# A causal mask moved: from a TensorE matmul into the score bank to a predicated copy on VectorE behind the exp

## The chip, the cores and the metric

The kernel runs on one NeuronCore of a Trainium2 chip. The metric is the time of one execution on the device in microseconds (us). The kernel before took 2042.52 us as the median of 3 runs (2041.71 to 2043.63).

## What is computed

One transformer block on a sequence of 2048 tokens of width 512, in float32: LayerNorm, attention with 32 query heads in 8 groups (4 query heads share one key and one value head, head size 64), residuals, LayerNorm, and a feed-forward part with ternary weights. The part that the change touches is this:

```python
q = _rope(q)
k = _rope(k)
qk = jnp.einsum('bghsd,bgxpd->bghsp', q, k) * DQK ** (-0.5)
causal = jnp.tril(jnp.ones((s, s), dtype=bool))
qk = jnp.where(causal, qk, -jnp.inf)
attn = jax.nn.softmax(qk, axis=-1)
o = jnp.einsum('bghsp,bgxpd->bghsd', attn, v)
```

## The kernel before, in words

There are four stages: `normalise` (to about 76 us), `attention` (about 76 to 1510 us), `output_projection` and `feed_forward`. The change lies in `attention` alone. Float32 values are split into a high and a low 16-bit half, and each product is made from several 16-bit matmuls.

**Tiling.** `attention` runs over 8 groups of heads. A group has 16 units: 4 chunks c of 512 queries, times 4 heads h. A unit has one step for each tile of 128 keys that its queries may see, so 4(c+1) steps; a group has 160 steps. In the last four steps of a unit (j = 4c to 4c+3) the key tile meets the queries on the diagonal: step 4c+r has only the query tiles r to 3, so 512, 384, 256 or 128 columns, and its first 128 columns need the causal mask. That makes 64 diagonal steps in a group: steps 0 to 15 (all of chunk 0), 20 to 23, 28 to 31, 36 to 39, 44 to 47 (chunk 1), 56 to 59, 68 to 71, 80 to 83, 92 to 95 (chunk 2), 108 to 111, 124 to 127, 140 to 143 and 156 to 159 (chunk 3). Over 8 groups there are 1280 steps, 512 of them diagonal.

**One step i.** TensorE makes the transposed scores (keys on partitions, queries on columns) in one of 2 score banks with two matmuls (L569, L570). In a diagonal step a third matmul (L573) adds, over 128 columns, `big` (30000 times the identity) times `mask_kq` (-30000 where key > query). ScalarE waits for that and writes the exp as float32 to `p32`, a ring of 10 (`exps`, L637). The upper 16 bits of each float32 are read in place as bfloat16 (`p_high`). GpSimd subtracts them and writes the float16 rest to `pl` (`low_part`, L789). TensorE multiplies both with the values (`values`, L586, L588, L590: three matmuls of 65, 64 and 65 columns for each query tile).

**Side work.** A softmax needs the row's maximum before its exp. TensorE makes the scores a second time, with queries on partitions, one piece of up to 512 columns a step (`max_piece`, L554), into 4 side banks in turn; VectorE reduces each piece (`reduce_piece`: L704 for whole pieces, L708 with the causal mask for those on the diagonal). Projections of later tokens (`project`, L541, 12 matmuls of 384 columns) share the 4 side banks; VectorE takes them out (`out_of_bank`, L727 to L733), GpSimd finishes rope and the low half (L795, L804). TensorE may write a side bank only when VectorE has read the item that was there four items before (`take_bank`).

**Order.** Every engine runs its own instructions in order. The order is written out by hand as slots, one for each step: in slot n TensorE does `scores(n)`, the slot's first piece, `values(n-5)`, and a projection if the slot has one (`JOB_STEPS`: among others slots 4, 8, 12 and 16). One slot later in the program order VectorE does its part: `unit_low`, `reduce_piece` of the slot, `unit_out`, `out_of_bank`. GpSimd does `low_part(n)`, then the rest of the projection's work. The first three steps of the next group (HEAD = 3) are scored at the end of a group, between the last three `values`, and their exp and `low_part` stand at the end of the slots; VectorE has `unit_out(15)` there. So in slot 3 of a group steps 0 to 2 are already done.

Of the kernel before, what the change touches and what calls it, by code (L numbers as in the profile page):

```python
# [226 lines left out]
    return max(0, j - TPC * c)  # L227


def score_bank(i):  # L230

    return i % SBANKS
# [110 lines left out]
def attention(nc, w_in_t, w_out_t, attn_dram, yh, yl, consts, cos, sin, wraw, wh, wl, wscale, raw, z_out):  # L343
# [6 lines left out]
    with ExitStack() as ctx:  # L350
        sb = lambda name, shape, dt: ctx.enter_context(nc.sbuf_tensor(name, shape, dt))
        sem = lambda name: ctx.enter_context(nc.semaphore(name))
        ident16, big, mask_kq, mask_qk = (consts[:, i, :] for i in range(4))
        rope_a = sb("rope_a", [P, TILES_KEPT, HG + 1, DH], F32)
        rope_b = sb("rope_b", [P, TILES_KEPT, HG + 1, DH], F32)
        qk_hi = sb("qk_hi", [P, 2, HG + 1, TPC, 2, DH], F16)
# [10 lines left out]
        o_hl = sb("o_hl", [P, 2, 2, TPC, HG, DH], F16)  # L367
        o_turn = sb("o_turn", [P, 2, 2, TPC, 2 * P], F16)
        credit = sb("credit", [P, 16], F32)
        causal = sb("causal", [P, CHUNK], BF16)  # L370
        masked = sb("masked", [P, 2, CHUNK], BF16)
        ps = ctx.enter_context(nc.psum_tensor("a_ps", [P, 8, 512], F32))
# [25 lines left out]
        maxs_used = sem("maxs_used")  # L398
        m_ready = sem("m_ready")
        exp_done = sem("exp_done")  # L400
        low_ready = sem("low_ready")
        pv_done = sem("pv_done")
        o_scaled = sem("o_scaled")
# [110 lines left out]
        def _(pe):  # L514
            pe.wait_ge(ones_set, 2)
            def group(g, par, part):
# [41 lines left out]
                def scores(i, ahead=0):  # L558
                    gg, side = g + ahead, par ^ ahead
                    u, j = step_of(i)  # L560
                    c, h = divmod(u, HG)
                    if j == 0:
                        pe.wait_ge(lm_in[c % 2][h], 16 * (2 * gg + c // 2 + 1))
                    pe.wait_ge(exp_done, gg * STEPS + bank_before(i) + 1 + EXP_AHEAD)
                    r = first_query_tile(c, j)
                    diag = j >= TPC * c
                    keys = slice(j * P, (j + 1) * P)
                    out = sbank(i)[:, r * P:CHUNK]
                    nc.tensor.matmul(out, k_hl[:, side, keys], q_hh[:, c % 2, h, r * P:CHUNK], start=True, stop=False)  # L569
                    last = nc.tensor.matmul(out, k_h1[:, side, keys], q_lm[:, c % 2, h, r * P:CHUNK],  # L570
                                            start=False, stop=not diag)
                    if diag:
                        last = nc.tensor.matmul(sbank(i)[:, r * P:(r + 1) * P], big, mask_kq, start=False, stop=True)  # L573
                    last.then_inc(scores_ready, 1)

                def values(i):
                    u, j = step_of(i)
# [103 lines left out]
        def _(dve):  # L681

            nc.vector.memset(v[:, :, :, DH:DH + 1], 1.0).then_inc(ones_set, 1)
            nc.vector.memset(causal[:, 0:CHUNK - P], 0.0)
            nc.vector.tensor_scalar(causal[:, CHUNK - P:CHUNK], mask_qk, LEAST / 3e4, None, ALU.mult).then_inc(causal_set, 1)
            dve.wait_ge(causal_set, 1)
# [4 lines left out]
            def group(g, par, part):  # L691
# [5 lines left out]
                def reduce_piece(ahead, u, i):  # L697
                    gg, (c, h), n = g + ahead, divmod(u, HG), FIRST_STEP[u] + i
                    t, kk = divmod(i, c + 1)
                    width = CHUNK if kk < c else (t + 1) * P  # L700
                    dve.wait_ge(maxs_ready, gg * PIECES + n + 1)
                    bank = side_bank(part, ("piece", ahead, u, i))[:, 0:width]
                    if kk < c:
                        nc.vector.reduce_max(mpart[:, u % 2, t, kk:kk + 1], bank, AX.X).then_inc(maxs_used, 1)  # L704
                    else:
                        if ahead or n >= 2:
                            dve.wait_ge(maxs_used, gg * PIECES + n - 1)
                        nc.vector.tensor_tensor_reduce(masked[:, n % 2, 0:width], bank, causal[:, CHUNK - width:CHUNK], 1.0, -LEAST,  # L708
                                                       ALU.add, ALU.max, mpart[:, u % 2, t, kk:kk + 1]).then_inc(maxs_used, 1)
                    if i < KEY_TILES[u] - 1:  # L710
                        return

                    dve.wait_ge(maxs_used, gg * PIECES + n + 1)
                    if ahead or c >= 2:
                        dve.wait_ge(lm_in[c % 2][h], 16 * (2 * gg + c // 2))
                    nc.vector.reduce_max(qk_lo[:, c % 2, h, :, 1, 0:1].rearrange("p t a -> p (t a)"),
                                         mpart[:, u % 2, :, 0:c + 1], AX.X).then_inc(m_ready, 1)

                def out_of_bank(ahead, t):
                    gg, side, b = g + ahead, par ^ ahead, t % TILES_KEPT  # L720
# [31 lines left out]
                for n in range(len(part) + 1):  # L752
                    step, _, pieces = slot(part, n - 1)
                    if step is not None and step - LOW_OUT_LAG in FIRST_STEP:
                        unit_low(FIRST_STEP.index(step - LOW_OUT_LAG) - 1)
                    for piece in pieces[:1]:
                        reduce_piece(*piece)
                    if step is not None and step - PV_LAG in FIRST_STEP[1:]:
                        unit_out(FIRST_STEP.index(step - PV_LAG) - 1)
                    for piece in pieces[1:]:  # L760
                        reduce_piece(*piece)
                    if step is not None:
                        if step in W_SPLIT and part is SLOTS:
                            weights_low(1, W_SPLIT[step])
                    if job := slot(part, n - OUT_OF_BANK_LAG)[1]:
                        out_of_bank(*job[1:])
                if part in (SLOTS, FINAL):
                    unit_out(UNITS - 1)
                if part is LAST:
# [6 lines left out]
        @block.gpsimd  # L776
        def _(pool):

            nc.gpsimd.memset(qk_lo[:, :, 0:HG, :, 1, :], 0.0).then_inc(rows_set, 1)
            nc.gpsimd.memset(qk_hi[:, :, HG, :, 1, 1:DH], 0.0).then_inc(rows_set, 1)  # L780
            nc.gpsimd.memset(qk_hi[:, :, HG, :, 1, 0:1], -1.0).then_inc(rows_set, 1)
            pool.wait_ge(ones_set, 2)
            def group(g, par, part):
                def low_part(i, ahead=0):
                    u, j = step_of(i)
                    r = first_query_tile(u // HG, j)
                    cols = slice(r * P, CHUNK)
                    pool.wait_ge(exp_done, (g + ahead) * STEPS + i + 1 + EXP_AHEAD)
                    nc.gpsimd.tensor_tensor(pl[:, i % RING, cols], p32[:, i % RING, cols], p_high[:, i % RING, cols],  # L789
                                            ALU.subtract).then_inc(low_ready, 1)  # L790

                def rope_sum(ahead, t):
                    b = t % TILES_KEPT
                    pool.wait_ge(rope_parts, (g + ahead) * TT + t + 1)
                    nc.gpsimd.tensor_tensor(rope_a[:, b], rope_a[:, b], rope_b[:, b], ALU.add).then_inc(roped_ready, 1)  # L795

                def qk_low_part(ahead, t):
                    (c, tt), gg = divmod(t, TPC), g + ahead
                    pool.wait_ge(qk_high, gg * TT + t + 1)
                    if tt == 0 and (ahead or c >= 2):  # L800
                        for h in range(HG):
                            pool.wait_ge(lm_in[c % 2][h], 16 * (2 * gg + c // 2))
                        pool.wait_ge(k_in[(c - 2) % NCH], 32 * (gg + (c >= 2)))
                    nc.gpsimd.tensor_tensor(qk_lo[:, c % 2, :, tt, 0, :], rope_a[:, t % TILES_KEPT], qk_hi[:, c % 2, :, tt, 0, :],  # L804
                                            ALU.subtract).then_inc(qk_low, 1)

                for n in range(len(part) + 2):
                    step = slot(part, n - 1)[0]
                    if step is not None:
                        if step >= HEAD:  # L810
                            low_part(step)
                    if job := slot(part, n - QK_LOW_LAG)[1]:
                        qk_low_part(*job[1:])
                    if job := slot(part, n - SUM_LAG)[1]:
                        rope_sum(*job[1:])
                for i in range(HEAD if part in (OPENING, SLOTS) else 0):
                    low_part(i, ahead=int(part is SLOTS))

            group(0, 0, OPENING)
            every_group(group)  # L820
# [400 lines left out]
def build(nc, x, w_in_t, w_out_t, rms_w, ffn_t, cos_dram, sin_dram, ident_dram, half_consts, out):  # L1221
    resid = nc.dram_tensor("resid_scratch", (S, D), F32, kind="Internal").ap()
    attn = nc.dram_tensor("attn_scratch", (2, TT, P, CT, P), F16, kind="Internal").ap()
    with nc.sbuf_tensor("raw", [P, NW], F32) as raw, nc.sbuf_tensor("ident_sb", [P, P], F32) as ident:
        with ExitStack() as ctx:
# [1 line left out]
            z_out = ctx.enter_context(nc.semaphore("z_out"))  # L1227
            yh = sb("yh", [P, KT, S], F16)
            yl = sb("yl", [P, KT, S], F16)
            consts = sb("consts", [P, 4, P], F16)  # L1230
            cos = sb("cos_sb", [P, TT, DH], F32)
            sin = sb("sin_sb", [P, TT, DH], F32)
            wraw = sb("wraw", [P, KT, GC], F32)
# [23 lines left out]
def shape_constants():  # L1257
# [4 lines left out]
    cos, sin = np.cos(ang).astype(np.float32), np.sin(ang).astype(np.float32)  # L1262
    big = np.float16(30000.0)
    key, query = np.arange(P)[:, None], np.arange(P)[None, :]
    half = np.stack([np.eye(P), np.eye(P) * big, np.where(key > query, -big, 0), np.where(query > key, -big, 0)], axis=1)
    unit = np.float32(QK_SCALE / W_SCALE)
    return (np.concatenate([cos, cos], 1) * unit, np.concatenate([-sin, sin], 1) * unit, np.eye(P, dtype=np.float32),
            half.astype(np.float16))
# [24 lines left out]
```

## Time and profile before

| | before |
|---|---|
| median of 3 runs | 2042.52 us |
| the profiled execution itself | 2040.19 us |
| its span, first to last instruction | 2038.3 us |
| TensorE busy | 1935.4 us (95%) |
| GpSimd busy | 1421.2 us (70%) |
| VectorE busy | 1234.5 us (61%) |
| ScalarE busy | 932.2 us (46%) |
| mean granted TensorE clock | 0.983 of full speed |

Busy times are unions of the durations of an engine's instructions. A matmul's duration includes the way through the array, so consecutive matmuls overlap in the record; what a matmul costs in a dense stream is the distance from its start to the next one's. The same holds, to a smaller degree, for VectorE, whose next instruction starts a little before the last one ends. The profile's stretches of time below are of group 4, which runs from 801.90 us (its first `scores`, in the tail of group 3) to 978.55 us.

### The profile page before, as it was taken

The numbers are of one execution on the slowest core, as the hardware profiler recorded it, in microseconds if no ns is written. First come the engines' busy times: TensorE is split into PE (matmuls) and PEld (weight loads), VectorE is DVE, ScalarE is ACT, GpSimd is POOL, SyncE is SP. The second block draws the span as 40 slices with busy tenths as digits, with TensorE's granted clock in tenths as the row PEclk, the third lists the DMA queues.
The fourth block names the chain that finished last, engine by engine and source line by source line (L and its number), as shares of the span: only waits on it lengthen the run. The fifth ranks groups of instructions, "written<-read, shape, count | busy, mean of one in ns | idle before, by whom it ended". The sixth has DMA issues, their size and how long they took to land. (4 is left out here: it accounts for less than half of the span.)

```text
span 2038.3 us, 55132 instructions
## 1 busy us (share of the span) xinstructions
PE 1935.4 (95%) x21382; PEld 1184.9 (58%) x21382; DVE 1234.5 (61%) x3284; ACT 932.2 (46%) x1969; POOL 1421.2 (70%) x1627
## 2 busy tenths in 40 slices
PE   4799989999999999999999999999969998999998
PEld 3466656666666666666666666666634443444443
DVE  6587558757866875886687588668625552121221
ACT  4355645555655555565555556555632211121110
POOL 1599979989999998999899899999930001131221
PEclk8799999999999999999999999999989999999999
DMA  6233263223224322322522332242246620000000
GB/s 205 58 66 46 46 158 65 46 50 76 44 53 87 61 46 55 71 46 51 98 51 46 59 66 46 51 81 52 38 155 227 217 83 1 16 5 21 5 16 21
DMA packets 301572, 136.79 MB, mean 67 GB/s; under 512 B 248336, under 2 KB 285456, under 8 KB 299792
## 3 DMA queue, kind: packets, MB, share of 16 engines
q1 hardware_dynamic: 301328, 133.43, 28.5%
q8 instruction: 166, 2.72, 0.6%
q14 instruction: 78, 0.64, 0.1%
HBM read 49.48 MB, written 25.17 MB: 37 GB/s over the span
## 5 line engine op out<-in xcount | busy, mean ns | idle before, releaser
L789 POOL TENSOR_TENSOR pl<-p 128x512 f16<-128x512 f32 (+3 forms) x1280 | 1136.3, 919 | 108.2 <-ACT p L637 107.0
L637 ACT ACTIVATE p<-a_ps 128x512 f32<-128x512 f32 (+3 forms) x1280 | 674.3, 532 | 606.1 <-PE a_ps L570 384.4
L704 DVE TENSOR_REDUCE mpart<-a_ps 128x1 f32<-128x512 f32 x768 | 514.2, 685 | 117.6 <-PE a_ps L554 114.7
L586 PE MATMUL a_ps<-v,p 128*128 128x65 f16 x4352 | 527.7, 193 | 14.9 <-POOL pl L789 11.3
L588 PE MATMUL a_ps<-v,p 128*128 128x64 f16 x4352 | 530.1, 194 | 0.0
L590 PE MATMUL a_ps<-v,pl 128*128 128x65 f16 x4352 | 526.9, 192 | 0.0
L586 PEld LDWEIGHTS a_ps<-v,p 128*128 128x128 bf16 x4352 | 412.1, 97 | 121.6 <-issue 16.8
L588 PEld LDWEIGHTS a_ps<-v,p 128*128 128x128 bf16 x4352 | 405.8, 97 | 103.2 <-issue 0.2
L554 PE MATMUL a_ps<-k_hl,q_hh 128*128 128x512 f16 (+3 forms) x1280 | 441.3, 350 | 24.6 <-issue 12.4
L569 PE MATMUL a_ps<-q_hh,k_hl 128*128 128x512 f16 (+3 forms) x1280 | 444.4, 347 | 2.5
L570 PE MATMUL a_ps<-q_lm,k_h 128*128 128x512 f16 (+3 forms) x1280 | 444.8, 347 | 0.0
L590 PEld LDWEIGHTS a_ps<-v,pl 128*128 128x128 f16 x4352 | 407.1, 99 | 0.0
L708 DVE CUSTOM_DVE_ANT_0 masked<-a_ps,causal 128x128 bf16<-128x128 f32 (+3 forms) x512 | 247.1, 484 | 81.5 <-PE a_ps L554 73.8
L1218 POOL TENSOR_TENSOR f_hl<-f_hid,f_hh 128x512 f16<-128x512 f32 x64 | 74.1, 1160 | 240.1 <-DVE f_hh L1188 240.1
L554 PEld LDWEIGHTS a_ps<-k_hl,q_hh 128*128 128x128 f16 x1280 | 124.0, 98 | 144.2 <-issue 16.9
L1133 PE MATMUL f_ps<-xh,tern 128*128 (+1 forms) x512 | 195.1, 381 | 1.8 <-DVE f_credit L1175 1.8
L1133 PE MATMUL f_ps<-xl,tern 128*128 (+1 forms) x512 | 195.0, 381 | 0.0
L541 PE MATMUL a_ps<-wh,yh 128*128 128x384 f16 x512 | 168.7, 329 | 8.6 <-DVE credit L690 8.6
L944 PE MATMUL p_ps<-p_wh,p_att 128*128 128x512 f16 x512 | 156.1, 381 | 14.9 <-DMA p_att<-attn_scratch 14.9
L541 PE MATMUL a_ps<-wl,yh 128*128 128x384 f16 x512 | 168.6, 329 | 0.0
L541 PE MATMUL a_ps<-wh,yl 128*128 128x384 f16 x512 | 168.4, 329 | 0.0
L1169 ACT ACTIVATE f_silu<-f_ps,tern_scale 128x512 f32<-128x512 f32 x64 | 44.0, 687 | 256.8 <-PE f_ps L1133 256.8
(96 smaller groups left out, 2268.2 us busy)
## 6 DMA issues: line engine op xcount, KB each, us to landing
attn_scratch<-o_turn SPq DMA_DIRECT2D x64, 256.0 KB, 2.8
p_att<-attn_scratch SPq DMA_DIRECT2D x32, 512.0 KB, 4.3
raw<-ffn_t SPq DMA_DIRECT2D x12, 1024.0 KB, 5.0
wraw<-w_in_t SPq DMA_DIRECT2D x8, 768.0 KB, 5.0
resid_scratch<-raw SPq DMA_DIRECT2D x4, 1024.0 KB, 4.3
raw<-w_out_t SPq DMA_DIRECT2D x1, 4096.0 KB, 16.8
x<-resid_scratch SPq DMA_DIRECT2D x4, 1024.0 KB, 7.5
out<-x SPq DMA_DIRECT2D x16, 256.0 KB, 2.1
```

Source lines behind the costliest of these rows:

```text
L541: last = nc.tensor.matmul(bank[:, 0:GC], a[:, kt, tok], b[:, kt, :], start=(kt == 0 and n == 0), stop=(kt == KT - 1 and n == 2))
L554: nc.tensor.matmul(bank[:, 0:width], q_hh[:, c % 2, h, t * P:(t + 1) * P], k_hl[:, par ^ ahead, kk * CHUNK:kk * CHUNK + width], start=True ...
L569: nc.tensor.matmul(out, k_hl[:, side, keys], q_hh[:, c % 2, h, r * P:CHUNK], start=True, stop=False)
L570: last = nc.tensor.matmul(out, k_h1[:, side, keys], q_lm[:, c % 2, h, r * P:CHUNK], start=False, stop=not diag)
L586: nc.tensor.matmul(o, weights, v[:, par, j, 0:VU], start=(j == 0 and t == 0), stop=False, skip_group_check=True)
L588: nc.tensor.matmul(o[:, 0:DH], weights, v[:, par, j, VL:VW], start=False, stop=False, skip_group_check=True)
L590: last = nc.tensor.matmul(o, pl[:, i % RING, t * P:(t + 1) * P], v[:, par, j, 0:VU], start=False, stop=(j == TPC * c + t), skip_group_chec ...
L637: nc.scalar.activation(p32[:, i % RING, r * P:CHUNK], sbank(i)[:, r * P:CHUNK], ACT.Exp, scale=SCALE).then_inc(exp_done, 1)
L704: nc.vector.reduce_max(mpart[:, u % 2, t, kk:kk + 1], bank, AX.X).then_inc(maxs_used, 1)
L708: nc.vector.tensor_tensor_reduce(masked[:, n % 2, 0:width], bank, causal[:, CHUNK - width:CHUNK], 1.0, -LEAST, ALU.add, ALU.max, mpart[:, ...
L789: nc.gpsimd.tensor_tensor(pl[:, i % RING, cols], p32[:, i % RING, cols], p_high[:, i % RING, cols], ALU.subtract).then_inc(low_ready, 1)
L1133: last = nc.tensor.matmul(bank, w[:, k, e * P:(e + 1) * P], x[:, k, bass.ds(c * CHUNK, CHUNK)], start=(k == 0 and x is xh), stop=(k == KT ...
```

## The change

The identity and `big` leave the constants, and so does the mask matmul of the diagonal steps. VectorE gets a tile of zeros, and for each diagonal step a predicated copy, `causal_cut`, which waits for the exp of the step and writes zeros to the 128 columns of `p32` where key > query (the predicate is the bit pattern of `mask_kq`, read as uint16). It stands in VectorE's order after `unit_low` and ahead of the slot's first `reduce_piece`; those of steps 0 to 2 stand after the slots, ahead of `unit_out(15)`. GpSimd's `low_part` of a diagonal step waits for the copy as well as for the exp. TensorE's `values` has no new wait: it waits for `low_part` already.

```diff
+def on_diagonal(i):
+    u, j = step_of(i)
+    return j >= TPC * (u // HG)
+
+def cuts_to(i):
+    return sum(on_diagonal(n) for n in range(i + 1))
+
+DIAGONALS = cuts_to(STEPS - 1)
...
-        ident16, big, mask_kq, mask_qk = (consts[:, i, :] for i in range(4))
+        mask_kq, mask_qk = (consts[:, i, :] for i in range(2))
...
+        zeros = sb("zeros", [P, P], F32)
+        future = mask_kq.bitcast(mybir.dt.uint16)
...
-                    diag = j >= TPC * c
...
-                    last = nc.tensor.matmul(out, k_h1[:, side, keys], q_lm[:, c % 2, h, r * P:CHUNK],
-                                            start=False, stop=not diag)
-                    if diag:
-                        last = nc.tensor.matmul(sbank(i)[:, r * P:(r + 1) * P], big, mask_kq, start=False, stop=True)
-                    last.then_inc(scores_ready, 1)
+                    nc.tensor.matmul(out, k_h1[:, side, keys], q_lm[:, c % 2, h, r * P:CHUNK],
+                                     start=False, stop=True).then_inc(scores_ready, 1)
...
+                def causal_cut(i, ahead=0):
+                    r = first_query_tile(step_of(i)[0] // HG, step_of(i)[1])
+                    dve.wait_ge(exp_done, (g + ahead) * STEPS + i + 1 + EXP_AHEAD)
+                    nc.vector.copy_predicated(p32[:, i % RING, r * P:(r + 1) * P], future, zeros[:, :]).then_inc(cut, 1)
...
                     if step is not None and step - LOW_OUT_LAG in FIRST_STEP:
                         unit_low(FIRST_STEP.index(step - LOW_OUT_LAG) - 1)
+                    if step is not None and step >= HEAD and on_diagonal(step):
+                        causal_cut(step)
                     for piece in pieces[:1]:
                         reduce_piece(*piece)
...
+                for i in range(HEAD if part in (OPENING, SLOTS) else 0):
+                    if on_diagonal(i):
+                        causal_cut(i, ahead=int(part is SLOTS))
                 if part in (SLOTS, FINAL):
                     unit_out(UNITS - 1)
...
                     pool.wait_ge(exp_done, (g + ahead) * STEPS + i + 1 + EXP_AHEAD)
+                    if on_diagonal(i):
+                        pool.wait_ge(cut, (g + ahead) * DIAGONALS + cuts_to(i))
                     nc.gpsimd.tensor_tensor(pl[:, i % RING, cols], p32[:, i % RING, cols], p_high[:, i % RING, cols],
                                             ALU.subtract).then_inc(low_ready, 1)
```

## Rows read from the trace of the kernel before

**Rows 1.** The page, busy time of engines, share of the span, instructions.
```profile
PE 1935.4 (95%) x21382; PEld 1184.9 (58%) x21382; DVE 1234.5 (61%) x3284; ACT 932.2 (46%) x1969; POOL 1421.2 (70%) x1627
```

**Rows 2.** Busy time by stretch: window, us, then busy us (instructions) of each engine.
```profile
804.00:820.00 16.00, 15.92 (x183) 10.65 (x181) 13.17 (x43) 8.43 (x24) 12.71 (x19) 1.00 0.32 61
820.00:835.00 15.00, 14.92 (x214) 10.28 (x213) 12.81 (x41) 10.46 (x25) 14.24 (x18) 1.00 0.40 89
835.00:880.00 45.00, 45.00 (x603) 30.00 (x601) 37.27 (x99) 26.64 (x61) 43.15 (x50) 1.00 0.42 78
880.00:963.70 83.70, 83.70 (x1138) 55.63 (x1137) 58.88 (x155) 46.47 (x98) 79.37 (x90) 1.00 0.22 38
963.70:981.00 17.30, 15.24 (x247) 10.54 (x246) 5.73 (x24) 10.56 (x24) 17.14 (x20) 1.00 0.52 99
```

**Rows 3.** Groups of instructions by line: busy, mean ns, idle before, releasers.
```profile
L789 POOL TENSOR_TENSOR pl<-p 128x512 f16<-128x512 f32 (+3 forms) x1280 | 1136.3, 919 | 108.2 <-ACT p L637 107.0
L573 PE MATMUL a_ps<-consts 128*128 128x128 f16 x512 | 112.5, 220 | 0.0
```

**Rows 4.** Timeline, TensorE: start us, us, instruction, idle before it.
```profile
802.33 0.22 PE L573 MATMUL a_ps<-consts 128*128 128x128 f16 x1
802.39 0.19 PE L586 MATMUL a_ps<-v,p 128*128 128x65 f16 x1
...
805.11 0.10 PEld L554 LDWEIGHTS a_ps<-k_hl,q_hh 128*128 128x128 f16 x1 [0.41 <-DVE mpart L704]
```

**Rows 5.** Timeline, VectorE in the normalisation, then at the group's start.
```profile
37.43 2.20 DVE L152 SCALAR_TENSOR_TENSOR wl<-wraw,wscale,wh 128x384 f16<-128x384 f32 x4
...
803.82 0.18 DVE L739 RECIPROCAL rden<-a_ps 128x4 f32<-128x4 f32 x1 [4.32 <-PE a_ps L590]
804.03 0.43 DVE L741 TENSOR_TENSOR a_ps<-a_ps,rden 128x256 f32<-128x256 f32 x1
804.38 0.68 DVE L704 TENSOR_REDUCE mpart<-a_ps 128x1 f32<-128x512 f32 x1
804.97 0.28 DVE L708 CUSTOM_DVE_ANT_0 masked<-a_ps,causal 128x128 bf16<-128x128 f32 x1
805.18 0.08 DVE L708 DVE_READ_ACCUMULATOR2_ANT mpart<- 128x1 f32 x1
805.18 0.69 DVE L704 TENSOR_REDUCE mpart<-a_ps 128x1 f32<-128x512 f32 x1
805.78 0.41 DVE L708 CUSTOM_DVE_ANT_0 masked<-a_ps,causal 128x256 bf16<-128x256 f32 x1
806.12 0.08 DVE L708 DVE_READ_ACCUMULATOR2_ANT mpart<- 128x1 f32 x1
```

**Rows 6.** VectorE's groups from 804 to 820 us, one row.
```profile
L727 DVE TENSOR_SCALAR v<-a_ps 128x64 f16<-128x64 f32 x3 | 0.7, 224 | 2.7 <-PE a_ps L541 2.7
```

**Rows 7.** Lines L694 and L152, durations min/median/max ns; timeline; GpSimd at 876.3, 877.5.
```profile
L694 DVE SCALAR_TENSOR_TENSOR wl<-wraw,wscale,wh x28: 710/818/1308, 151.2 to 1236.0; 128x384 f16<-128x384 f32 x28
...
L152 DVE SCALAR_TENSOR_TENSOR wl<-wraw,wscale,wh x4: 609/613/614, 37.4 to 39.0; 128x384 f16<-128x384 f32 x4
...
876.23 1.30 DVE L694 SCALAR_TENSOR_TENSOR wl<-wraw,wscale,wh 128x384 f16<-128x384 f32 x1
...
L789 POOL TENSOR_TENSOR pl<-p 128x512 f16<-128x512 f32 x1 | 1.0, 1035 | 0.0
...
L789 POOL TENSOR_TENSOR pl<-p 128x512 f16<-128x512 f32 x1 | 1.4, 1351 | 0.0
```

**Rows 8.** Timeline, GpSimd and ScalarE around the group's start and end.
```profile
802.59 1.52 ACT L637 ACTIVATE p<-a_ps 128x512 f32<-128x512 f32 x3 [3.04 <-PE a_ps L573]
...
803.26 3.75 POOL L789 TENSOR_TENSOR pl<-p 128x512 f16<-128x512 f32 x5 [0.17 <-ACT p L637]
808.43 0.83 POOL L789 TENSOR_TENSOR pl<-p 128x384 f16<-128x384 f32 x1 [1.42 <-ACT p L637]
...
813.42 0.83 POOL L789 TENSOR_TENSOR pl<-p 128x384 f16<-128x384 f32 x1 [1.42 <-ACT p L637]
...
963.70 1.04 POOL L789 TENSOR_TENSOR pl<-p 128x512 f16<-128x512 f32 x1 [0.72 <-ACT p L637]
...
971.01 8.74 POOL L789 TENSOR_TENSOR pl<-p 128x512 f16<-128x512 f32 x10
```

More of the change, by code:

```diff
@@ L400, in attention @@
         exp_done = sem("exp_done")
+        cut = sem("cut")
         low_ready = sem("low_ready")
@@ L683, in _ @@
             nc.vector.memset(v[:, :, :, DH:DH + 1], 1.0).then_inc(ones_set, 1)
+            nc.vector.memset(zeros[:, :], 0.0)
             nc.vector.memset(causal[:, 0:CHUNK - P], 0.0)
@@ L1229, in build @@
             yl = sb("yl", [P, KT, S], F16)
-            consts = sb("consts", [P, 4, P], F16)
+            consts = sb("consts", [P, 2, P], F16)
             cos = sb("cos_sb", [P, TT, DH], F32)
@@ L1264, in shape_constants @@
     key, query = np.arange(P)[:, None], np.arange(P)[None, :]
-    half = np.stack([np.eye(P), np.eye(P) * big, np.where(key > query, -big, 0), np.where(query > key, -big, 0)], axis=1)
+    half = np.stack([np.where(key > query, -big, 0), np.where(query > key, -big, 0)], axis=1)
     unit = np.float32(QK_SCALE / W_SCALE)
```

## The prediction

> **What bounds the kernel now.** I read the page's busy shares first [rows 1]: TensorE 95%, GpSimd 70%, VectorE 61% over the whole span. These are averages over stages, so the second view is busy time by stretch for one group of the attention [rows 2]. There TensorE is busy nearly all the time from 804 to 963.7 us, GpSimd is close behind it (12.71 + 14.24 + 43.15 + 79.37 = 149.47 of 159.7 us), and VectorE, harmless on the page, is busy 13.17 of 16.0 us and 12.81 of 15.0 us in the first two stretches, 83% of 31 us. The third view is the waits. GpSimd idles only for the exp, 108.2 us in all [rows 3], and each exp it waits for had itself waited for TensorE; it idles 1.42 us at 808.43 and at 813.42, after a projection has kept TensorE from scores [rows 8]. From 963.70 to the group's end GpSimd has no gap, with ten `low_part` in a row from 971.01 [rows 8], and TensorE is busy only 15.24 of 17.3 us [rows 2]. So a group is bound by TensorE for some 160 us and by GpSimd for the last 17 us. VectorE already touches TensorE once: at 805.11 the piece of slot 4 waits 0.41 us for the reduce that began at 804.38 [rows 4, 5].
>
> **What is removed.** 512 mask matmuls [rows 3]. Their recorded 220 ns is mostly the way through the array; in the stream one costs 802.39 - 802.33 = 0.056 us (to the rounding of these rows) [rows 4]. That is 64 x 0.056 = 3.6 us a group and 29 us in all if TensorE were the bound everywhere. The masks of steps 156 to 159 and 0 to 2 lie where GpSimd is the bound, so at most 57 x 0.056 = 3.2 us a group, 25.5 us in all. The exp's operand and time stay.
>
> **What VectorE gets.** The trace has no predicated copy. The nearest operation has both inputs in SBUF like it (zeros and predicate) and float32 in it: L152, four in 2.20 us with the last 0.613 us long, so one per (2.20 - 0.61)/3 = 0.53 us at 384 columns [rows 5, 7]. By columns: L708 takes 0.21 us to the next start at 128 and 0.34 us at 256 [rows 5], so 0.13 us for 128 columns, and 0.53 - 0.26 = 0.27 us at 128. The lower bound is the 0.21 us of L708. I take 0.27 us.
>
> **What the copy waits for.** The same operation as L152 runs in the attention as L694, beside a working GpSimd, and takes 710 to 1308 ns, median 818, where L152 takes 609 to 614 [rows 7]. The slowest kind shows how: L694 starts at 876.23 while GpSimd is in a subtraction of 1035 ns, ends at 877.53, and the next GpSimd subtraction takes 1351 ns, against 1035 for its neighbour. VectorE stood still until GpSimd's instruction ended, then GpSimd stood still until VectorE's ended. The mean of L694 is about 0.3 us over L152. A copy of 128 columns is as likely to meet a running GpSimd instruction, so the added wait lies between 0 (GpSimd idle, or the copy's operands don't meet GpSimd's) and 1.04 us (a whole L789), and I take 0.3 us where GpSimd is saturated. Where VectorE is late, GpSimd itself is waiting for the copy and partly idle, and I take 0.2 us. GpSimd loses 1351 - 1035 = 0.316 us to 384 columns; less 0.26 for the smaller width that is 0.05 us for each copy.
> The Trainium skill (SBUF — State Buffer, section Who interferes with whom) says that a VectorE instruction with two SBUF inputs contends with a GpSimd instruction that reads SBUF, the loser blocking for the whole instruction. This trace agrees (1305 and 1351 ns above). The page doesn't list the predicated copy there; if the rule holds for it, the sum below stands, and if not, the first rival does.
>
> **The sum for one group, by stretch.** VectorE's demand is its busy time [rows 2] plus the copies.
> (a) 804 to 820 us, slots 3 to 16, 13 copies. VectorE has 2.83 us idle, 2.7 of it waiting for projections [rows 6]. 13 x (0.27 + 0.2) = 6.1 us don't fit. Two things happen. First, copies 0 to 2 stand ahead of `unit_out(15)` and of slot 0's reduce. The exps of steps 0 to 2 run from 802.59 to 804.11 [rows 8], and copy 1 or 2 also meets GpSimd's subtractions of 1.04 us; so the reduce that began at 804.38 begins at about 805.7. TensorE was waiting for just that one in slot 4 [rows 4], so it loses 1.3 us directly. Second, VectorE falls behind by 0.27 + 0.2 us a diagonal slot and recovers in the projections; the four side banks let it be about 2 us late without harm. 13.17 + 6.1 = 19.3 us in 16; of the 3.3 us too much about 1.7 are carried. I take +1.6 us.
> (b) 820 to 835 us, slots 17 to 31, 8 copies, GpSimd busy 14.24 of 15: 12.81 + 8 x 0.57 = 17.4 us, +2.4 us.
> (c) 835 to 880 us, 16 copies: 37.27 + 16 x 0.57 = 46.4 us of 45, +1.4 us, part of it the lag carried in.
> In (a) to (c) VectorE is the bound, and the masks' 0.056 us come back as longer waits of TensorE.
> (d) 880 to 963.7 us, 20 diagonal steps: 58.88 + 20 x 0.57 = 70.3 us of 83.7, it fits. GpSimd 79.37 + 20 x 0.05 = 80.4, it fits too. TensorE saves 20 x 0.056 = 1.1 us: -1.1 us.
> (e) 963.7 to 981 us, GpSimd's stretch, 7 copies: VectorE is idle two thirds of it and makes the copies in time (GpSimd lags the exp), but each costs GpSimd 0.05 us, and `low_part(0)`, which waited 0.17 us for the exp [rows 8], now waits for a copy behind it: +0.5 us.
> Together 1.6 + 2.4 + 1.4 - 1.1 + 0.5 = +4.8 us a group, times 8 = +38 us. The profiled execution took 2040.2 us (span 2038.3 and 1.9 around it), so 2078.6; the runs' median lies 2.3 us above it: 2081 us.
>
> **What costs nothing.** The smaller constants, the memset of the zeros before the first group, the removed weight loads (beside matmuls). ScalarE's exp starts 0.056 us sooner, which only lengthens GpSimd's backlog.
>
> **Rivals.**
> 1. The copy doesn't meet GpSimd's reads: no 0.2 to 0.3 us. Then (a) 13.17 + 3.5 = 16.7 us of 16 with a carry, so 0 to +0.7; (b) 12.81 + 2.2 = 15.0 of 15, 0; (c) 37.27 + 4.3 = 41.6 of 45, -0.9; (d) -1.1; (e) 0. That is -1.3 to -2.0 us a group, up to the -3.2 us of all masks: 2017 to 2032, about 2028 us. For it: VectorE has 39% idle on the page, and only L694, 28 instructions, speaks for the blocking. Against: L694 is never as fast as L152 in 28 cases. It decides from about 0.1 us of blocking for each copy: then (a) and (b) give 1.3 + 0.7 us back, as much as (c) and (d) save.
> 2. TensorE's saving and VectorE's lateness cancel, or GpSimd swallows both: GpSimd has only 159.7 - 149.5 = 10 us of gaps in the 160 us that TensorE bounds, and where it has none (820 to 835 us) a faster TensorE gains nothing. 2038 to 2047, about 2043 us.
> 3. The blocking is worse than L694's mean, since GpSimd's next instruction is always the one that has just been released: 0.6 us. Then (a) +4, (b) 12.81 + 7.0 = 19.8, +4.8, (c) 37.27 + 13.9 = 51.2, +6.2, (d) -1.1, (e) +1: +15 us a group, 2162 us at the extreme. Against: a VectorE that late leaves GpSimd idle, which ends the blocking. I take 2115 us and up as this case.
> That the mask isn't applied as said is no rival: the copy is issued once for each diagonal step.
>
> **Chances.** My case (VectorE becomes the bound in the first half of a group) 0.62, of itself 2050 to 2112; rival 1 0.22; rival 2 0.08; rival 3 0.08. Faster by over 0.2% (what can be told from no change here, 4 us): 0.22. Within: 0.08. Slower: 0.70. The range must reach into rival 1: 2030 to 2112 leaves out about half of it and rival 3.
>
> **What would show it.** Right: the predicated copy's row has a mean well over 0.28 us and a maximum near 1.3 us; TensorE's L554 has a wait for VectorE's L704 or L708 of some us a group, most in slots 4 to 31, where it is 0.41 us at one place now; VectorE's idle before L727 shrinks; GpSimd waits for the copy instead of the exp in the first 20 us of a group; the stretch from step 0 to step 72 grows by 5 us and that from 880 to 963.7 shrinks by 1. Wrong: copies of 0.2 to 0.3 us without spread (rival 1), or a slow group whose lost time lies in GpSimd's stretch at the end, which I price at 0.5 us, or a longer time with VectorE idle in slots 0 to 31: then the new wait for the exp in VectorE's queue, not its load, is the cause.

## The result, and the profile after

The kernel after takes 2091.82 us (median of 4 runs, 2089.49 to 2096.55); the kernel before took 2042.12 us beside it. The ratio is 1.0249, with a 95% interval of 1.0230 to 1.0268: 49.7 us slower. The prediction was 2081 us, in a range of 2030 to 2112, with a chance of 0.70 for slower. The profiled execution took 2089.49 us, its span 2087.7 us.

The page's first part and the two groups that answer to [rows 1] and [rows 3] (busy us, mean ns of one, idle before, releaser):

```profile
PE 1927.7 (92%) x20870; PEld 1155.9 (55%) x20870; DVE 1443.1 (69%) x3797; ACT 929.2 (45%) x1969; POOL 1442.5 (69%) x1627
...
L816 POOL TENSOR_TENSOR pl<-p 128x512 f16<-128x512 f32 (+3 forms) x1280 | 1150.3, 925 | 135.6 <-DVE p L737 69.4
...
L737 DVE COPY_PREDICATED p<-consts,zeros 128x128 f32<-128x128 uint16 x512 | 275.2, 539 | 83.7 <-ACT p L650 80.8
```

TensorE has 512 matmuls less and is busy 7.7 us less; the time is 50 us more, so it waits more. VectorE is busy 208.6 us more (0.41 us for each copy), and GpSimd idles 27 us more in front of its subtractions, now half of the time for the copy. A copy takes 539 ns on average, though 128 columns are short work. The durations of that line (min/median/max) show a wide spread:

```profile
L737 DVE COPY_PREDICATED p<-consts,zeros x512: 287/459/1192, 77.7 to 1540.1; 128x128 f32<-128x128 uint16 x171
```

Busy time by stretch in group 4, cut at the same steps as [rows 2] (window, length, then TensorE, its weight loads, VectorE, ScalarE, GpSimd, granted clock):

```profile
826.30:843.90 17.60, 16.20 (x177) 10.56 (x176) 17.34 (x57) 8.29 (x24) 13.20 (x18) 1.00 0.24 47
843.90:860.40 16.50, 14.74 (x199) 9.19 (x197) 15.71 (x46) 9.99 (x24) 16.50 (x21) 1.00 0.35 74
860.40:908.20 47.80, 44.68 (x584) 28.96 (x584) 45.07 (x116) 26.71 (x61) 42.10 (x49) 1.00 0.43 76
908.20:992.70 84.50, 83.07 (x1117) 54.69 (x1116) 67.69 (x180) 46.49 (x98) 80.65 (x90) 1.00 0.20 38
992.70:1011.60 18.90, 16.47 (x239) 10.93 (x238) 8.36 (x30) 10.60 (x24) 17.47 (x21) 0.91 0.45 92
```

Where TensorE was busy without a break it now is not, and VectorE is busy 17.34 of 17.60 us, 15.71 of 16.50 us and 45.07 of 47.80 us: up to about step 72 it has next to no room. In the second stretch GpSimd has none at all (16.50 of 16.50 us), so there busy time doesn't say which of the two is the bound. The longest waits of TensorE in the first and the third stretch of group 4 are one in slot 4, which the prediction named, and one in slot 32, which it did not (timeline, idle time before in brackets):

```profile
828.70 0.39 PE L571 MATMUL a_ps<-k_hl,q_hh 128*128 128x512 f16 x1 [1.40 <-DVE mpart L718]
...
861.83 0.38 PE L571 MATMUL a_ps<-k_hl,q_hh 128*128 128x512 f16 x1 [2.28 <-issue]
```

The first is the wait that was 0.41 us long in [rows 4] on the weight load, and was said to grow by 1.3 us. The second has no name in the view. The last key transpose before it was issued at 859.26 us and landed 2.5 us later, and the matmul starts 0.09 us after the landing:

```profile
k_hl<-qk_lo SPq DMA_TRANSPOSE x1, 2.5
```

In all eight groups this piece starts 0.09 us after that landing, after a wait of 2.28 to 3.51 us. In groups 1 to 6 it is 2.98 us on average; in the kernel before, it was 0.83 us on average, and nothing in group 4. VectorE ahead of the wait in slot 4, to be laid beside [rows 5]:

```profile
825.66 0.31 DVE L737 COPY_PREDICATED p<-consts,zeros 128x128 f32<-128x128 uint16 x1 [2.66 <-ACT p L650]
826.15 1.36 DVE L737 COPY_PREDICATED p<-consts,zeros 128x128 f32<-128x128 uint16 x2 [0.19 <-ACT p L650]
827.42 0.17 DVE L759 RECIPROCAL rden<-a_ps 128x4 f32<-128x4 f32 x1
827.62 0.43 DVE L761 TENSOR_TENSOR a_ps<-a_ps,rden 128x256 f32<-128x256 f32 x1
827.97 0.68 DVE L718 TENSOR_REDUCE mpart<-a_ps 128x1 f32<-128x512 f32 x1
```

The reciprocal stood at the head of VectorE's queue; now three copies do, which wait for the exps (2.66 and 0.19 us) and, the last two, for GpSimd (1.36 us for two).

A table of the whole, from the starts of the exps of the steps named, mean of groups 1 to 6, in us. The four later columns are the difference to before:

| steps | before | after | no_mask_matmul | aside_load_only | copies_late_only |
|---|---|---|---|---|---|
| 3 to 16 | 16.96 | +1.10 | -0.78 | +0.09 | -0.13 |
| 16 to 32 | 15.57 | +1.53 | 0.00 | -0.01 | +0.01 |
| 32 to 72 | 45.85 | +2.69 | -0.87 | +1.27 | +0.04 |
| 72 to 145 | 82.67 | +0.80 | -0.77 | +0.99 | -0.61 |
| 145 to 3 of the next | 18.11 | +0.28 | -0.18 | 0.00 | +0.01 |
| sum | 179.16 | +6.39 | -2.60 | +2.34 | -0.68 |

Within 72 to 145, the kernel after is +1.40 in steps 72 to 84 and -0.61 in 84 to 144. Not every row is the same in each group. In steps 3 to 16 the kernel after loses 1.54 us in four of the six groups, group 4 among them, and nothing in group 1. In steps 32 to 72 the losses of single groups of one kernel lie up to 3.7 us apart, so a mean there is worth less than one in another row. The +0.28 of the last row is 0.05 or less in five groups and 1.57 in group 4, where the granted clock fell (see the end).

### The profile page after: what moved, and what is told of

The parts are those of the page before. It is cut to its first block and busy times, and to the rows that moved or that the text cites. A ratio compares the mean times of both kernels' runs of the same rounds, so it can differ in the third digit from the quotient of the medians.

```text
span 2087.7 us, 55133 instructions
## 1 busy us (share of the span) xinstructions
PE 1927.7 (92%) x20870; PEld 1155.9 (55%) x20870; DVE 1443.1 (69%) x3797; ACT 929.2 (45%) x1969; POOL 1442.5 (69%) x1627
## 5 line engine op out<-in xcount | busy, mean ns | idle before, releaser
L816 POOL TENSOR_TENSOR pl<-p 128x512 f16<-128x512 f32 (+3 forms) x1280 | 1150.3, 925 | 135.6 <-DVE p L737 69.4
L718 DVE TENSOR_REDUCE mpart<-a_ps 128x1 f32<-128x512 f32 x768 | 506.9, 681 | 38.7 <-PE a_ps L571 37.3
L737 DVE COPY_PREDICATED p<-consts,zeros 128x128 f32<-128x128 uint16 x512 | 275.2, 539 | 83.7 <-ACT p L650 80.8
```

The costliest lines, as they stand in the source:

```text
L737: nc.vector.copy_predicated(p32[:, i % RING, r * P:(r + 1) * P], future, zeros[:, :]).then_inc(cut, 1)
```

## The experiments

The theory under test: a copy makes VectorE late, by its load and most of all by standing blocked behind GpSimd's running instruction; TensorE then waits for side banks. The rivals were that GpSimd's new wait for the copy costs the time, and that the wait for the exp at the head of VectorE's queue does. Each kernel was timed beside the kernel before (2041.49 us in the first four, 2041.56 in the next four, 2040.57 in the next three, 2039.74 in the last).

### One SBUF input instead of two

```diff
-nc.vector.copy_predicated(p32[:, i % RING, r * P:(r + 1) * P], future, zeros[:, :]).then_inc(cut, 1)
+nc.vector.reduce_max(aside[:, i % 16:i % 16 + 1], p32[:, i % RING, r * P:(r + 1) * P], AX.X).then_inc(cut, 1)
```

> The kernel after, with the predicated copy replaced by a max-reduce of the same 128x128 float32 tile of p32 into a spare column: same place in VectorE's order, same waits for the exp, GpSimd still waits for it, but one SBUF input instead of two and hardly a write. The mask is left out of the weights. Theory (the copy is blocked behind GpSimd's running instruction): each takes about 0.28 us without spread, GpSimd's 128x512 subtractions have none of 1.08 to 1.09 us beside it, and the time falls from 2092 to 2030-2050 us. Rival (the load of 512 more instructions and their wait for the exp at the head of VectorE's queue cost the time, whatever the operands): 2075-2095 us.

Measured: 2059.17 us, ratio 1.0080 (1.0063 to 1.0097). The operation in the copy's place:

```profile
L737 DVE TENSOR_REDUCE aside<-p x512: 266/278/288, 77.0 to 1512.6; 128x1 f32<-128x128 f32 x171
its engine sat idle before it (us, times) until:
  ACT p L650: 98.0, 110
```

No spread, as the theory said, and 32.7 us of the kernel's time are gone. But the time missed my 2030 to 2050: 17.7 us over before are left, and against the kernel without masks (2022.06) even 37.1. Load and waits cost more than I gave them. The reduce also writes only one column, so this run alone doesn't say whether the second input or the wide write made the copy wait. The kernel after has an operation that does: the first product of rope reads PSUM and one SBUF input, and writes 320 float32 columns to SBUF.

```profile
L749 DVE TENSOR_TENSOR rope_a<-a_ps,cos_sb x128: 473/481/483, 49.0 to 1443.0; 128x320 f32<-128x320 f32 x128
```

Of these 128, 103 started while a GpSimd instruction ran (95 of them a `low_part`), and none is longer than 483 ns. So a wide float32 write beside GpSimd costs nothing here, and what the blocked operations share (the copy, and the weight split of [rows 7]) is the second SBUF input.

### No mask at all

```diff
-                    if diag:
-                        last = nc.tensor.matmul(sbank(i)[:, r * P:(r + 1) * P], big, mask_kq, start=False, stop=True)
```

> The kernel before with the 512 mask matmuls left out and nothing in their place, so the scores of the weights have no causal mask. It prices what the change can save on TensorE. Theory: TensorE bounds about 57 of 64 diagonal steps of a group, but GpSimd has few gaps there, so 1.3 to 2.5 us a group of the possible 3.6: 2022-2032 us. Rival (GpSimd swallows it): 2038-2043 us.

Measured: 2022.06 us, ratio 0.9900 (0.9883 to 0.9916), -19.4 us. The saving is real, 2.4 us a group of the 3.6 in the stream. By the table it comes from steps 3 to 16 and from all after 32. Nothing comes from 16 to 32, where GpSimd is busy 14.92 of 15.57 us (810.50 to 826.07 us of that trace).

### The copies aside, with nobody waiting for them

```diff
+                def causal_cut(i, ahead=0):
+                    dve.wait_ge(exp_done, (g + ahead) * STEPS + i + 1 + EXP_AHEAD)
+                    n = cuts.pop()
+                    cuts.append(n + 1)
+                    if n >= 4:
+                        dve.wait_ge(cut, n - 3)
+                    nc.vector.copy_predicated(aside[:, n % 4], future, zeros[:, :]).then_inc(cut, 1)
```

> The kernel before with its mask matmuls, plus the 512 predicated copies in the place that the change gives them, waiting for the exp, but into a tile of their own; nobody waits for them. Theory (VectorE's load, with the blocking behind GpSimd, makes TensorE wait for side banks): most of the loss is there, 2080-2100 us. Rival (GpSimd's new wait for the copy is the loss): 2043-2055 us.

Measured: 2106.40 us, ratio 1.0320 (1.0302 to 1.0337), +64.9 us; 6 us over my range. GpSimd's new wait is not the main loss: without it, and with TensorE's masks back, the time is longer than that of the kernel after. One stretch is an exception: in steps 16 to 32 this kernel loses 0.69 us a group and the kernel after 1.53, and the masks are worth nothing there; so about half of the loss in that stretch comes only when GpSimd waits for the copy.

### Load, blocking and the wait for the exp, one by one

The same kernel without the wait for the exp, and then with a reduce of a constant tile in place of the copy:

```diff
-                    dve.wait_ge(exp_done, (g + ahead) * STEPS + i + 1 + EXP_AHEAD)
```

> As copies_aside (kernel before, masks on TensorE, 512 predicated copies into a tile of their own, nobody waits for them), but the copies don't wait for the exp: load and blocking behind GpSimd stay, the wait at the head of VectorE's queue goes. Theory (load, blocking and the wait each carry a share; in copies_aside VectorE idles 80 us in front of the copies for the exp): 2065-2088 us, against 2106 with the wait. Rival (the wait costs nothing, the idle time would be spent anyway): 2100-2108 us.

```diff
-                    nc.vector.copy_predicated(aside[:, n % 4], future, zeros[:, :]).then_inc(cut, 1)
+                    nc.vector.reduce_max(aside[:, n % 4, 0:1], zeros[:, :], AX.X).then_inc(cut, 1)
```

> As aside_no_exp_wait, with each copy replaced by a max-reduce of a constant 128x128 float32 tile: 0.28 us of VectorE each, one SBUF input, no wait for the exp, so VectorE's load alone. Theory: 512 x 0.21 us in the stream is 13 us a group, which fits into the 31 us of idle time in most stretches: 2042-2055 us. Rival (VectorE's load by itself is what costs the 37 us of one_sbuf_input): 2068-2080 us.

Measured: 2095.96 us (ratio 1.0268, 1.0253 to 1.0284) and 2056.53 us (1.0068, 1.0053 to 1.0084). The two lines, min/median/max:

```profile
L738 DVE COPY_PREDICATED aside<-consts,zeros x512: 284/538/1192, 78.4 to 1540.2; 128x128 f32<-128x128 uint16 x171
```

```profile
L737 DVE TENSOR_REDUCE aside<-zeros x512: 268/276/283, 78.3 to 1503.9; 128x1 f32<-128x128 f32 x171
```

So the wait for the exp costs 10.4 us (I expected 18 at least: a miss by 8), and the blocking is the large part: 2095.96 - 2056.53 = 39.4 us. The load alone costs 15.0 us, 1.5 us over the top of what I had expected.

### The copy behind the slot's reduces

```diff
-                    if step is not None and step >= HEAD and on_diagonal(step):
-                        causal_cut(step)
                     for piece in pieces[:1]:
                         reduce_piece(*piece)
...
                     for piece in pieces[1:]:
                         reduce_piece(*piece)
+                    if step is not None and step >= HEAD and on_diagonal(step):
+                        causal_cut(step)
```

> The kernel after with each copy behind the slot's reduces instead of ahead of the first one; loads are the same. Theory (VectorE's load is the bound): TensorE gets its banks earlier but GpSimd its copy later, and the load stays, so the time stays within 15 us of 2092: 2080-2105 us. Rival (the wait for the exp at the head of VectorE's queue, ahead of reduces that were ready, is the loss): 2045-2070 us.

Measured: 2111.44 us, ratio 1.0338 (1.0321 to 1.0355), 20 us more than the kernel after; 6 us over my range. The waits for the exp shrink, the others grow (groups as in [rows 3], and the longest waits):

```profile
L737 DVE COPY_PREDICATED p<-consts,zeros 128x128 f32<-128x128 uint16 x512 | 326.9, 643 | 27.2 <-ACT p L650 26.2
```

```profile
POOL pl L816 <- DVE p L737: 87.1, 186, 1.4
```

VectorE idles 26 us for the exp, not 81, but a copy takes 643 ns instead of 539, and GpSimd waits longer for it. That the copy now more often comes in the middle of a GpSimd instruction is my reading of the 643 ns.

### The copies of steps 0 to 2 behind unit_out

```diff
-                for i in range(HEAD if part in (OPENING, SLOTS) else 0):
-                    if on_diagonal(i):
-                        causal_cut(i, ahead=int(part is SLOTS))
                 if part in (SLOTS, FINAL):
                     unit_out(UNITS - 1)
+                for i in range(HEAD if part in (OPENING, SLOTS) else 0):
+                    if on_diagonal(i):
+                        causal_cut(i, ahead=int(part is SLOTS))
```

> The kernel after with the copies of steps 0 to 2 of the next group behind unit_out(15) instead of ahead of it. In the kernel after TensorE waits 1.40 us for VectorE's reduce in slot 4 (group 4). Theory (copies wait for the exps of steps 0 to 2 while unit_out could run): the wait of slot 4 falls by up to 0.5 us, the length of unit_out, and the time by 2-7 us: 2085-2090 us. Rival (the three copies cost the same wherever they stand ahead of slot 0's reduce): 2090-2094 us.

Measured: 2094.88 us, ratio 1.0259 (1.0243 to 1.0275). No gain over 2091.82, a hair outside the rival's range. By the exps, steps 3 to 16 are 0.6 us a group shorter than in the kernel after, and steps 32 to 72 are 1.6 us longer: what is saved at one place is waited for further on.

### Copies only where VectorE has room, and only where it has none

```diff
+def by_copy(i):
+    return on_diagonal(i) and 84 <= i < 144
...
-                    diag = j >= TPC * c
+                    diag = on_diagonal(i) and not by_copy(i)
```

> Both masks in one kernel: predicated copies (and no mask matmul) for the diagonal steps 84 to 143 of a group, 16 of 64, where the kernel after is shorter than before by 0.18 + 0.02 + 0.22 + 0.19 us by stretch; mask matmuls and no copy for the others. Theory: VectorE has idle time there, so the saving is kept and nothing is lost: 0.6 us a group, 2035-2039 us, under the kernel before by 0.2%. Rival (VectorE's lateness is handed on to later slots in any case): 2041-2050 us.

Measured: 2039.03 us, ratio 0.9983 (0.9974 to 0.9993), 10 runs. This version beats both kernels, but only by 0.1 to 0.3% (2.5 us between the medians). The table shows the saving where it was expected (-0.61 in steps 72 to 145) and nothing lost elsewhere in groups 1 to 6. Times eight that would be 4.9 us; the last group loses 1.4 us instead, and steps 32 to 72 scatter. The other half has `0 <= i < 84`:

> The other half of copies_late_only: predicated copies for the diagonal steps 0 to 83 of a group (48 of 64), mask matmuls for steps 84 to 159. Theory (the whole loss lies in the steps 0 to 83, where VectorE is full, and the later copies save a little): 50.3 + 2.5 = 53 us over before, 2090-2098 us. Rival (the loss is spread over all copies, 48/64 of it here): 2076-2082 us.

Measured: 2097.68 us, ratio 1.0275 (1.0260 to 1.0291), 57 us over before. The loss isn't spread over the copies: the 48 of steps 0 to 83 make all of it.

```diff
-    return on_diagonal(i) and 84 <= i < 144
+    return on_diagonal(i) and (84 <= i < 144 or 56 <= i < 60)
```

> copies_late_only with the four diagonal steps 56 to 59 by copy as well (20 of 64). Theory (what a copy costs depends on the place: these four stand where VectorE isn't late when no copy has come before, so they save 4 x 0.056 = 0.22 us a group and cost nothing later): 2036-2038 us. Rival (slots 60 to 72 follow at once, with VectorE's four weight splits that are blocked behind GpSimd like the copies; VectorE is late there and TensorE waits for side banks): 2042-2052 us.

Measured: 2053.92 us, ratio 1.0071 (1.0057 to 1.0085). A clear miss of the theory, and 2 us over the rival's range too: four copies more in a group cost 2.40 us in steps 60 to 72, where I had them save 0.22. This is the best place to see one copy and GpSimd together. VectorE and GpSimd in steps 56 to 59 of group 4 (timeline):

```profile
871.28 0.41 DVE L778 TENSOR_TENSOR o_hl<-a_ps,o_hl 128x256 f16<-128x256 f32 x1
871.62 1.18 DVE L746 COPY_PREDICATED p<-consts,zeros 128x128 f32<-128x128 uint16 x1
872.70 0.41 DVE L731 CUSTOM_DVE_ANT_0 masked<-a_ps,causal 128x256 bf16<-128x256 f32 x1
873.05 0.08 DVE L731 DVE_READ_ACCUMULATOR2_ANT mpart<- 128x1 f32 x1
873.05 1.09 DVE L746 COPY_PREDICATED p<-consts,zeros 128x128 f32<-128x128 uint16 x1
874.05 1.27 DVE L727 TENSOR_REDUCE mpart<-a_ps 128x1 f32<-128x512 f32 x2
875.24 0.77 DVE L746 COPY_PREDICATED p<-consts,zeros 128x128 f32<-128x128 uint16 x1
...
876.40 0.53 DVE L746 COPY_PREDICATED p<-consts,zeros 128x128 f32<-128x128 uint16 x1
```

```profile
870.60 2.04 POOL L825 TENSOR_TENSOR pl<-p 128x512 f16<-128x512 f32 x2
872.94 1.04 POOL L825 TENSOR_TENSOR pl<-p 128x512 f16<-128x512 f32 x1 [0.30 <-DVE p L746]
874.28 0.83 POOL L825 TENSOR_TENSOR pl<-p 128x384 f16<-128x384 f32 x1 [0.30 <-DVE p L746]
```

The copy that starts at 871.62 ends at 872.80, 0.16 us after GpSimd's subtractions end at 872.64; GpSimd, which needs that copy, goes on at 872.94. The next copy starts at 873.05 beside that subtraction, which ends at 873.98, and ends at 874.14, again 0.16 us later; GpSimd goes on at 874.28. The two engines work in turn: each of the four copies waits for a running GpSimd instruction, and GpSimd's next subtraction for the copy. The four copies take about 3.6 us of VectorE in place of 1.1. TensorE pays in three waits, at 874.78, 879.55 and 886.16 us (its waits from 868 to 890 us, summed):

```profile
PE a_ps L576 <- DVE mpart L727: 1.1, 2, 0.7
PE a_ps L576 <- DVE mpart L731: 0.5, 1, 0.5
```

The kernel with copies at 84 to 143 only has no such wait there, but VectorE is busy 22.41 of 25.00 us (865 to 890 us). The theory had looked at VectorE's lateness in these four steps, and left out the work that follows them: four weight splits, which are blocked behind GpSimd like the copies. The rival had named just these.

### Key transposes sooner in SyncE's queue

```diff
-        timed.append((n + QK_LOW_LAG + 4, ("k", c, 0, ahead)))
+        timed.append((n + QK_LOW_LAG + 2.25, ("k", c, 0, ahead)))
```

> The kernel after with the two key transposes of a chunk placed 1.75 slots earlier in SyncE's order, ahead of the query_low transpose that waits for VectorE's row maxima; nothing else changes. In the kernel after TensorE waits 2.3 to 3.5 us at the first piece of slot 32, with no releaser that the profile names. Theory (VectorE's lateness reaches that piece by way of SyncE's queue: maxima late, query_low late, keys behind it late): the wait of slot 32 falls by 1.3 us or more in each group, 2076-2086 us. Rival (the piece waits for a side bank or for TensorE's own code): 2090-2094 us.

> copies_late_only with the same move of the key transposes. There the wait of slot 32 is 0.6 to 1.6 us. Theory: it goes by 0.5 us or more in each group, 2030-2036 us, under the kernel before (2041.5) by 0.3% to 0.5%. Rival: no change, 2038-2040 us.

Measured: 2094.99 us (ratio 1.0269, 1.0254 to 1.0285) and 2072.02 us (1.0159, 1.0145 to 1.0173). Both miss. The first is no faster than the kernel after, as the rival said, though not for the rival's reason. The second is 33 us slower than `copies_late_only`, where a gain was expected. In the kernel after, SyncE's queue before slot 32 is (issue, then the duration):

```profile
855.39 1.19 SPq L459 DMA_TRANSPOSE q_lm<-qk_lo  x1
856.68 1.21 SPq L450 DMA_TRANSPOSE q_hh<-qk_hi  x1
857.98 1.22 SPq L467 DMA_TRANSPOSE k_h<-qk_hi  x1
859.26 1.26 SPq L467 DMA_TRANSPOSE k_hl<-qk_lo  x1
```

The first starts 0.08 us after VectorE has written the maxima that it needs, and the rest follow in a row. With the keys first, the wait without a name in slot 32 has names:

```profile
860.94 0.39 PE L585 MATMUL a_ps<-q_hh,k_hl 128*128 128x512 f16 x1 [0.73 <-DMA q_lm<-qk_lo]
863.00 0.47 PE L571 MATMUL a_ps<-k_hl,q_hh 128*128 128x512 f16 x1 [1.46 <-DMA q_hh<-qk_hi]
```

So VectorE's lateness does reach slot 32 through SyncE's queue, as the landing of `k_hl` showed above, but the queue is full at that place: four transposes of 1.2 us, all wanted at slot 32, and whichever is put first, the others are late. Nor can the keys start much sooner: in this trace GpSimd finishes their low half at 855.44 us, and their first transpose starts at 855.51. The remedy of my theory falls. In the version with late copies the move breaks two places that had been in order: 1.58 us a group more in steps 16 to 32, where TensorE waits for `q_lm`, and 2.21 us in steps 72 to 84, where it waits for `q_hh`.

## Why the prediction was right

**TensorE's saving: as said.** 25.5 us at most, 19.4 us measured by itself. The kernel after gets its part only from step 84 on, 0.61 us a group; (d) had it at 1.1 for steps 80 to 143.

**The price of a copy: right in kind, a little too high.** 0.27 us in the stream and 0.2 to 0.3 us blocked gave 0.47 to 0.57 us. The mean duration is 0.539 us, the minimum 0.287 us, the maximum 1.19 us, so the blocking is 0.25 us on average, as said. But the next instruction starts about 0.1 us before a copy ends (0.20 us after the start of an unblocked one, at 829.37 us), and VectorE's busy time grew by 0.41 us a copy. That the waiting is GpSimd's instruction is shown by the ends: all 331 copies that took over 350 ns end 0.155 to 0.175 us after the GpSimd instruction that ran when they started, and the 71 that started with GpSimd idle took 0.287 to 0.311 us. Of the 110 others, 103 started in the last 0.182 us of a GpSimd instruction and 7 within 0.11 us of its start; those 7 weren't held up (0.295 to 0.299 us). The reduce without spread says the same.
The Trainium skill (SBUF — State Buffer, section Who interferes with whom) has the rule for instructions with two SBUF inputs; the copies behave by it, with 1.18 us where 0.29 us is the length without a neighbour. That it is the second input and not the write is shown by the rope product above (at most 483 ns beside GpSimd).

**The parts of the loss.** From pairs of kernels: masks out -19.4 us, load +15.0, blocking +39.4, the wait for the exp +10.4. That is +45.4 of the 49.7 measured, if the parts may be added; the rest, 4.3 us, is GpSimd's wait for the copy and whatever the parts do to each other, and wasn't tried by itself. Rival 1 (no blocking, about 2028 us) fell with its premise, and even one_sbuf_input, which has none, took 2059 us: this rival was priced too well too, since it gave the load and the wait for the exp nothing.

**By stretch.** (a) +1.6 was +1.10, (b) +2.4 was +1.53, (e) +0.5 was +0.28 us, of which 0.25 is the clock in group 4. (a) held in its mechanism to the wait: 1.40 us in slot 4 in place of 0.41, and +1.54 us in group 4, from which it was worked out. (e) did not: without the clock nearly nothing is lost there. The mis-sized terms are (c), +1.4, measured +2.69, and (d), -1.1, measured +0.80, so (d) had the wrong sign: together 3.2 us a group too little, 25 us in all, against 1.6 us a group too much in (a), (b) and (e). Both were sums of VectorE's demand over a long window, and TensorE doesn't wait for sums.

(c) left out two waits. One is slot 32's wait for the key transpose, 2.98 us against 0.83 before, which VectorE's busy time doesn't contain. The other is the ground behind step 56, where the kernel after loses 1.67 us up to step 72 and, in (d), 1.40 us more up to step 84. There TensorE waits four times for VectorE's reduces in group 4 (timeline):

```profile
900.07 0.39 PE L571 MATMUL a_ps<-k_hl,q_hh 128*128 128x512 f16 x1 [0.76 <-DVE mpart L722]
...
906.68 0.39 PE L571 MATMUL a_ps<-k_hl,q_hh 128*128 128x512 f16 x1 [0.85 <-DVE mpart L718]
...
909.76 0.39 PE L571 MATMUL a_ps<-k_hl,q_hh 128*128 128x512 f16 x1 [0.62 <-DVE mpart L718]
...
911.36 0.39 PE L571 MATMUL a_ps<-k_hl,q_hh 128*128 128x512 f16 x1 [0.78 <-DVE mpart L718]
```

VectorE has its four weight splits there, and they are blocked behind GpSimd like the copies (median of all 28 in the kernel 1150 ns, 818 before). In (d) its demand fits into the whole window, as said (67.69 of 84.50 us busy), but from 908.2 to 923.0 us it is busy 13.49 of 14.80 us. The load alone, without any blocking of its own, already costs 0.98 to 0.99 us in steps 72 to 84 in each of the groups 1 to 6. Only behind step 84, with VectorE busy 54.20 of 69.70 us, is there the saving that (d) had from step 72 on. This is also the sign that failed: the stretch from 880 us on did not shrink by 1 us.

**The range.** The time lies in the range because it reached up to 2112, and because errors of both signs partly cancelled. Over all eight groups the profiled executions differ by 48.3 us (the first and the last group lose 4.8 and 5.2 us, the six between 6.39 on average), where the sum had 38.4. That is 9.9 of the 10.8 us between 2081 and 2091.8; the rest is less than executions of one kernel differ by.

## What to carry to other kernels

Before work is moved from a busy engine to one that looks 39% idle, look at its idle time in stretches as short as its buffers are deep (here four banks), and at whether the new instruction has two inputs in SBUF beside an engine with which it then has to take turns; here that made 0.3 us of work 0.54, and where the neighbour also waits for the result, 0.9. A mechanism with the right sign in one part of the order (steps 84 to 143) can be kept there alone: that gave 2.5 us where the whole change lost 50. A wait that the profile gives no name can be laid beside the landings of the DMAs. And in a full queue a reordering only changes who waits.

## What the runs showed of the hardware

- A 128x128 float32 predicated copy with its predicate (uint16) and source in SBUF takes 0.29 us by itself. Beside a running GpSimd instruction it ends 0.155 to 0.175 us after that one (331 copies), up to 1.19 us after its own start. The blocking needs no dependence: copies into a tile of their own show the same (284/538/1192 ns). A VectorE product with one SBUF input that writes 320 float32 columns to SBUF shows none of it (473/481/483 ns).
- GpSimd loses less in return: a 128x512 subtraction that began before the end of such a blocked copy takes 1.082 to 1.097 us (123 cases), against a median of 1.040 us for the others.
- The granted clock was 0.91 in the last stretch of group 4 (992.7 to 1011.6 us) in the kernel after, 0.76 from 1005 to 1010 us, so at the lower level (1.2 GHz) for a part of it; it was 1.00 in the same stretch before. TensorE had waited there five times for GpSimd or ScalarE, 0.16 to 0.52 us each, but it has four such waits in the same stretch before, so the cause stays open. From the exp of step 144 to that of step 3 of the next group it took 22.6 us against 21.1 in the other groups: 1.5 us went that way in this one group.
